# Layer two's node pass of a four-layer graph network: the reciprocal root of the variance from a ScalarE guess and two Newton steps on VectorE, in place of GpSimd's power

## The reference, cut to what matters

```python
def _layernorm(x, axis=-1, eps=1e-05):
    m = jnp.mean(x, axis=axis, keepdims=True)
    v = jnp.var(x, axis=axis, keepdims=True)
    return (x - m) / jnp.sqrt(v + eps)
...
    x = _layernorm(x + _L2_gnn_ref(x, src, dst, L2_gnn_W, L2_gnn_attn_l, L2_gnn_attn_r), axis=-1)
...
    # in _L2_gnn_ref: return jax.nn.elu(out.reshape(n, H * D))
    # in _L3_gnn_ref, the first steps:
    h = (x @ W.T).reshape(N, H, C)
    a_s = jnp.einsum('nhc,hc->nh', h, att_src)
    a_d = jnp.einsum('nhc,hc->nh', h, att_dst)
```

## Time and profile before

| | before |
|---|---|
| median of three runs, us | 5578.91 |
| lowest and highest, us | 5576.49, 5587.16 |
| profiled execution: span, us | 5581.5 |
| PE busy | 4162.6 us, 75% |
| DVE (VectorE) busy | 3702.1 us, 66% |
| POOL (GpSimd) busy | 3611.4 us, 65% |
| ACT (ScalarE) busy | 1962.3 us, 35% |
| power L1604 and scatters L1610 of the pass | 49 and 392 instructions |

### The profile page before, as it was taken

How to read it: one execution, slowest core, us unless ns; L and a number is a source line. 1 busy time by engine, 2 the same in 40 slices (tenths; PEclk the granted TensorE clock), 3 DMA queues, 4 the chain that set the end, 5 groups by cost and what they waited for, 6 DMA issues and landing times. The chain is left out here.

```text
span 5581.5 us, 69994 instructions
## 1 busy us (share of the span) xinstructions
PE 4162.6 (75%) x16758; PEld 2810.8 (50%) x16758; DVE 3702.1 (66%) x10203; ACT 1962.3 (35%) x3345; POOL 3611.4 (65%) x3319
## 2 busy tenths in 40 slices
PE   2276679999999999999999977776877500036666
PEld 1154445556666666666666667665666400012222
DVE  2155456666666666666666667777999665568887
ACT  0011135532222222222222222226888400026666
POOL 7488654443555556555555567775888777768887
PEclk7689889999999999999999988887999855569988
DMA  9988789985433333333333244447999733359998
GB/s 376 294 153 156 148 263 366 364 329 186 149 124 120 119 127 123 120 117 124 122 117 116 84 133 138 138 136 255 351 348 351 248 95 94 95 181 343 357 344 289
DMA packets 497175, 1129.62 MB, mean 202 GB/s; under 512 B 164007, under 2 KB 246907, under 8 KB 497031
## 3 DMA queue, kind: packets, MB, share of 16 engines
q1 hardware_dynamic: 331530, 866.20, 44.4%
q0 software_dynamic: 113184, 174.84, 12.9%
q10 hardware_dynamic: 52316, 87.06, 4.5%
HBM read 627.40 MB, written 543.83 MB: 210 GB/s over the span
## 5 line engine op out<-in xcount | busy, mean ns | idle before, releaser
L1067 PE MATMUL psum<-W2b,arena 128*128 128x256 f32 x3136 | 725.4, 380 | 0.0
L799 DVE TENSOR_SCALAR arena<-arena 128x256 f32<-128x256 f32 x784 | 462.6, 651 | 366.3 <-POOL arena L794 361.8
L1048 PE MATMUL psum<-arena,W1b 128*128 128x512 f32 x1568 | 699.2, 599 | 0.0
L1067 PEld LDWEIGHTS psum<-W2b,arena 128*128 128x128 f32 x3136 | 574.6, 191 | 65.2 <-issue 0.5
L1761 PE MATMUL psum<-arena,ident 128*128 128x512 f32 x784 | 409.9, 672 | 208.1 <-POOL arena L1819 206.0
L959 ACT ACTIVATE arena<-psum,hbias 128x512 f32<-128x512 f32 x392 | 269.4, 687 | 821.2 <-PE psum L1048 821.2
L1048 PEld LDWEIGHTS psum<-arena,W1b 128*128 128x128 f32 x1568 | 290.6, 190 | 401.7 <-issue 401.7
L1192 POOL DMA_INDIRECT tab<-arena,IDX x392 | 405.1, 1033 | 122.8 <-issue 91.5
L790 POOL TENSOR_TENSOR arena<-arena,lneps 128x4 f32<-128x4 f32 x196 | 41.5, 212 | 670.1 <-DVE arena L786 669.1
L1610 POOL DMA_INDIRECT ad_d<-arena,FE x392 | 394.6, 1007 | 114.3 <-issue 113.7
L917 POOL DMA_INDIRECT xd_d<-arena,FE x360 | 378.1, 1050 | 99.8 <-issue 96.9
(11 more groups left out here) (256 smaller groups left out, 9286.1 us busy)
## 6 DMA issues: line engine op xcount, KB each, us to landing
arena<-tab SPq DMA_DIRECT2D x194, 544.0 KB
arena<-x_d SPq DMA_DIRECT2D x202, 512.0 KB, 7.0
arena<-in_x SPq DMA_DIRECT2D x194, 512.0 KB, 4.8
x_d<-arena SPq DMA_DIRECT2D x194, 512.0 KB, 2.9
tab<-zero SPq DMA_DIRECT2D x11, 5832.0 KB, 54.9
tab<-blank SPq DMA_DIRECT2D x97, 544.0 KB
h_d<-arena SPq DMA_DIRECT2D x97, 528.0 KB, 6.0
arena<-h_d SPq DMA_DIRECT2D x97, 528.0 KB, 5.5
```

Source lines behind the costliest of these rows:

```text
L799: v.tensor_scalar(y[:, j, :], r[:, j, :], self.mv[:, j, 0:1], self.rs[:, j:j + 1], ALU.subtract, ALU.mult).then_inc(self.s["y"], 1)
L1048: last = pe.matmul(psum[:, HB[c], :], W1b[:, f, c * P:(c + 1) * P], x1T[:, f, :], start=False, stop=(f == FH - 1))
L1067: last = pe.matmul(outB(j), hid[:, c, j * P:(j + 1) * P], W2b[:, c, :], start=(c == 0), stop=(c == KH - 1))
```

## The change

The power leaves GpSimd. VectorE now writes `half` = (variance + epsilon) / 2 for a pair (in place of `ve`). ScalarE makes a first guess of the reciprocal root: it reads the bits of `half` as an integer, which is near a linear function of the logarithm, and takes the exponential of that times -ln 2 / 2^24 plus a constant `logb`. VectorE improves the guess in `shift` by two steps of the form r = r x (half x r x r - 1.5), three instructions each, every one waiting for the one before by the semaphore `small`. The sign turns with each step and is right after two. The semaphore counts of the last pass are moved to match.

```diff
--- before.py
+++ after.py
@@ -98,6 +98,9 @@
     BIG = 1.0e30
     LN_EPS = 1e-5
     SLOPE = 0.2
+    LN2 = 0.6931471805599453
+
+    LOGB = 0.5 * LN2 * (127 - 0.043 - 1.0)
 
     NS = -(-N // STEP)
     NLAST = (N - (NS - 1) * STEP) // J
@@ -1474,7 +1477,9 @@
             y = take([NB, J, D])
             st = take([J, 6])
             mv = take([2, 2 * J, 2])
-            ve = take([2 * J])
+            half = take([2, 2 * J])
+            t1 = take([2 * J])
+            logb = take([1])[:, 0:1]
             rsd = take([2, 2 * J])
             nm = take([2, 2 * J])
             gap = take([1])
@@ -1483,7 +1488,7 @@
             cursor[0] = max(cursor[0], ahead["edge_end", 2])
             xt = take([NB, J, D])
             unit = psum[:, 6:8, :].rearrange("p a (j d) -> p (a j) d", d=D)
-            r = dict(nodes, **nodes2)
+            r = dict(nodes, small=nodes3["small"], **nodes2)
             assert NS % 2 == 0 and NB == 4
 
             def out_wait(eng, k):
@@ -1581,9 +1586,16 @@
                     wait(act, r["mm"], 2 * (k.s - 1))
                     for f in range(FH):
                         act.activation(xT[:, k.slot(2), f, :], psum[:, f, :], ACT.Copy).then_inc(r["xT"], 1)
+                def guess(k):
+                    b = k.slot(NB) // 2
+                    act.wait_ge(r["ve"], k.turn(2) + 2)
+                    wait(act, r["nm"], k.turn(2) - 1)
+                    act.activation(rsd[:, b, :], half[:, b, :].bitcast(I32), ACT.Exp, bias=logb, scale=-LN2 / 2 ** 24).then_inc(r["rs"], 1)
                 relu_exp(beat(0, NB))
 
                 def body(k):
+                    if k.slot(2) == 0 and not (k.known() and k.s == 0):
+                        guess(k.plus(-2))
                     if live(k.plus(1), NS):
                         relu_exp(k.plus(1))
                     if not (k.known() and k.s < 2):
@@ -1591,18 +1603,13 @@
                     if not (k.known() and k.s < 3):
                         evac(k.plus(-3))
                 run_beats(act, NS, body, NB, peel=2 * NB)
+                guess(beat(NS - 2, NB))
                 for s in range(NS - 2, NS):
                     normed(beat(s, NB))
                     evac(beat(s - 1, NB))
                 evac(beat(NS - 1, NB))
 
             def n_gpsimd(pool):
-                def rstd(p):
-                    wait(pool, r["y"], J * (2 * p - 2))
-                    wait(pool, r["nm"], p - 1)
-                    pool.wait_ge(r["ve"], p + 1)
-                    pool.tensor_tensor(out=rsd[:, p % 2, :], in0=ve, in1=expo[:, :], op=ALU.pow).then_inc(r["rs"], 1)
-
                 def to_edges(k):
                     pool.wait_ge(r["hs"], 2 * (k.s + 1))
                     for j in range(J):
@@ -1610,8 +1617,6 @@
                         pool.indirect_dma_start(out=ad_d[:, :], out_offset=bass.IndirectOffsetOnAxis(ap=FE[:, c:c + 1], axis=0),
                                                 in_=hs[:, k.slot(NB), j, D + H3:HW], in_offset=None, bounds_check=EP - 1, oob_is_err=False).then_inc(s_xd[k.slot(NB)], 16)
                 for s in range(NS):
-                    if s % 2 == 1:
-                        rstd(s // 2)
                     if s > 4:
                         to_edges(beat(s - 5, NB))
                 for s in range(NS - 5, NS):
@@ -1631,9 +1636,16 @@
 
                 def shift(k):
 
-                    b = k.slot(NB) // 2
-                    v.wait_ge(r["rs"], k.turn(2) + 1)
+                    b, p = k.slot(NB) // 2, k.turn(2)
+                    v.wait_ge(r["rs"], p + 1)
                     wait(v, r["y"], J * (k.s - 2))
+                    for i in range(2):
+                        v.tensor_tensor(out=t1, in0=rsd[:, b, :], in1=half[:, b, :], op=ALU.mult).then_inc(r["small"], 1)
+                        v.wait_ge(r["small"], 6 * p + 3 * i + 1)
+                        v.tensor_tensor(out=t1, in0=t1, in1=rsd[:, b, :], op=ALU.mult).then_inc(r["small"], 1)
+                        v.wait_ge(r["small"], 6 * p + 3 * i + 2)
+                        v.scalar_tensor_tensor(out=rsd[:, b, :], in0=t1, scalar=-1.5, in1=rsd[:, b, :], op0=ALU.add, op1=ALU.mult).then_inc(r["small"], 1)
+                        v.wait_ge(r["small"], 6 * p + 3 * i + 3)
                     v.scalar_tensor_tensor(out=nm[:, b, :], in0=mv[:, b, :, 0], scalar=-1.0, in1=rsd[:, b, :], op0=ALU.mult, op1=ALU.mult).then_inc(r["nm"], 1)
 
                 def body(k):
@@ -1660,10 +1672,10 @@
                         v.bn_aggr(mv[:, k.slot(NB) // 2, b * J + j, :], st[:, j, :]).then_inc(r["mv"], 1)
                     if b == 1:
                         v.wait_ge(r["mv"], J * (k.s + 1))
-                        wait(v, r["rs"], k.turn(2))
-                        v.tensor_tensor(out=ve, in0=mv[:, k.slot(NB) // 2, :, 1], in1=lneps[:, :], op=ALU.add).then_inc(r["ve"], 1)
+                        v.tensor_scalar(half[:, k.slot(NB) // 2, :], mv[:, k.slot(NB) // 2, :, 1], LN_EPS, 0.5, ALU.add, ALU.mult).then_inc(r["ve"], 1)
                     if not (k.known() and k.s < 4):
                         to_rows(k.plus(-4))
+                v.memset(logb, LOGB).then_inc(r["ve"], 1)
                 run_beats(v, NS, body, NB, peel=NB + 1)
                 shift(beat(NS - 2, NB))
                 for s in range(NS - 4, NS):
@@ -1824,7 +1836,7 @@
                     pool.wait_ge(r["mv"], J * (k.s + Z + 1))
                     pool.tensor_tensor(out=ve, in0=mv[:, b, :, 1], in1=lneps[:, 0:J], op=ALU.add).then_inc(r["ve"], 1)
                     wait(pool, r["y"], J * (k.s + Z - 1))
-                    pool.wait_ge(r["ve"], k.s + ZP + 1)
+                    pool.wait_ge(r["ve"], k.s + ZP + 2)
                     pool.tensor_tensor(out=rsd[:, b, :], in0=ve, in1=expo[:, 0:J], op=ALU.pow).then_inc(r["rs"], 1)
                     pool.wait_ge(r["rs"], k.s + ZP + 1)
                     pool.wait_ge(r["neg"], k.s + 1)
@@ -1842,7 +1854,7 @@
                 def factors(k):
 
                     p = k.turn(2)
-                    c0 = 6 * p
+                    c0 = 6 * (p + ZP)
                     for n in (k, k.plus(1)):
                         b = n.slot(NB)
                         v.wait_ge(gd[b], 16 * (n.turn(NB) + GD[b] + 1))
```

## The result

The changed kernel takes 5613.78 us (median of four runs, 5605.57 to 5618.13) against 5583.03 us of the kernel before in the same comparison (5576.49 to 5588.44). The ratio is 1.0056 with an interval of 1.0041 to 1.0070: 31 us slower, between 23 and 39. The forecast was 5603, 24 more, in a range of 5590 to 5622. A second comparison gave 1.0055 (1.0041 to 1.0069). The profiled execution's span grew from 5581.5 to 5616.4 us.

What follows compares the result with a forecast made beforehand. The prediction took GpSimd to bound the changed pass, VectorE close behind. Steps +60.5, waits given back -29.3 and tail -7.2 sum to +24.0 us; on the median 5578.9 that gives 5603, range 5590 to 5622.

Steps and rivals of the forecast that it cites:

- The bound: In the changed pass's loop GpSimd never waits and sets the pace; VectorE has only 1.15 us to spare in four beats.
- The price of the steps: Six chained 128x8 VectorE instructions in front of L1637 for each of 48 pairs, 0.21 us each: +60.5 us.
- The waits given back: VectorE's waits for GpSimd's power in the changed pass disappear: -29.3 us.
- The tail: At the pass's end GpSimd is behind with its scatters; without the power they end earlier: -7.2 us.
- ScalarE and TensorE at 0: The guess's place in ScalarE's order makes neither evacuation nor matmuls late in the loop; slack about 1.0 us, cost 0.
- What was to be seen: Changed profile: turn about 25.9 us, steps 0.21 apart, GpSimd idle some 0.9 a beat, last scatter about 7 after last L1634.
- Rival A: The six steps flow like independent instructions, 0.07 us apart: not slower, -16 us, 5563; chance 6%.
- B: The loop's register instructions make each Newton step instruction cost 0.30 us: +50 us, 5629; chance 8%.
- C: The guess in ScalarE's order makes evacuation and matmuls late, so VectorE's L1629 waits: 48 us more, 5651; chance 7%.
- Rival D: VectorE's Newton steps and GpSimd's scatters hold each other in the loop: 125 us more, 5728; chance 2%.
- The argument against D: L1853, L1855 and L1858 start 0.22 to 0.23 us apart beside GpSimd's power, so instructions with two SBUF inputs aren't held.
- the likeliest case: Whole kernel with step pitches of 0.20 to 0.23 us (+21 to +30) and a tail gain of 5 to 8: 5598 to 5611.

## Why the prediction was right, and where it was not

- **The bound.** Right: GpSimd set the pace, VectorE had 1.15 us a turn to spare. The kernel without steps shows the 23.42 as 23.40.
- **The price of the steps.** 0.21 each was taken, 0.20 measured. 48 x 6 x 0.20 = 57.6 for 60.5: this term was 3 us too large and is most of what the pass fell short of the forecast. Taken by the kernel without steps it is 658.0 - 602.8 = 55.2. A turn was to be 25.94 and is 25.81.
- **The waits given back.** -29.3 fits: 57.6 - 29.3 - 6.4 (the tail, next point) = 21.9 for 21.3 measured. No run shows it alone. The kernel without steps shows it together with a tail: 602.8 - 636.7 = -33.9, where -29.3 - 7.2 = -36.5 was forecast. By that run this part was too large by 2.6 and the steps by 5.3, and the two errors cancel in part.
- **The tail.** From the last variance to the last scatter's end it was 4433.08 - 4399.28 = 33.8 us and is 4456.10 - 4428.65 = 27.5: -6.4 where -7.2 was forecast, and the gap between the last L1634 and the end is 8.2 for some 7. GpSimd started beat 93's scatters at 4430.85, 0.8 after L1634's end at 4430.08, where I had it start at once; a scatter of the beat before was under way until 4430.17. The kernel with the unused power takes 5.1 of the gain back.
- **ScalarE and TensorE at 0.** Right, and shown alone by the guess in the old kernel (635.9 against 636.7). The guess itself is 0.30, not the 0.23 of the nearest row.
- **What was to be seen.** Right but for GpSimd's idle time: it waits for L1634 43.1 us in the 36 beats of the stretch above, 1.2 a beat, where the text said 0.9; its own terms, 25.94 / 4 - 5.2, give 1.3.
- **Rival A** (0.07 apart) described instructions that don't depend on each other, and these exist: 0.077. The Newton steps are a chain and don't behave so. B and C did not occur. **Rival D** did not occur in this pass: the longest L1643 of 98 is 0.242 us, although more than half of the pass's small VectorE instructions start while a scatter runs.
- **The argument against D was wrong in its breadth.** From one place in the last pass I concluded that the trace disagrees with the Trainium skill ("SBUF — State Buffer", Who interferes with whom), by which a VectorE instruction with two SBUF inputs and a GpSimd one that reads SBUF exclude each other for a whole instruction. L1853 and L1855, two of the very lines I cited, are held for 1.8 us in the profile of before that was at hand (4963.75 and 4965.61), behind the product L1819. The rule agrees with the trace for that product. It does not for the power: in the last pass of that profile 314 VectorE instructions of 128x32 start beside one and take 0.193 (median), and with the unused power 15 of 128x8 start beside it and take at most 0.169. Nor does it for the scatters. The sum was not touched, as only these two run here.
- **The total.** 31 us for 24. The missing part is no term of the sum: the 10 us outside the changed pass, which the profiles place in the last pass. I priced its edits at nothing and left them unnamed among the risks; whether they are its cause is open. 5613.8 lies above the 5598 to 5611 of the likeliest case. That it is in the range is in part luck: the upper part of the range was meant for half of rival B and the spread of runs, and something else filled it.

## What to carry to other kernels

Before work is moved off the engine that sets the pace, read how much the next engine has to spare in one turn of the loop: the gap was 0.58 us a pair here, and a chain of six small instructions, 1.2 us, could not fit into it although each is tiny. Price small instructions by whether they wait for each other (0.20 us here) or not (at most 0.08), and shorten the chain or give each engine a part of the pairs rather than move all of it. An engine that comes out of a loop behind its work leaves a tail, and what waits at a fixed place in its order makes it fall behind even when it has time.

## What the runs showed of the hardware that was not expected

- Six VectorE products of 128x8 started 0.077 us apart when independent, and cost the loop only 0.035 each; in a chain they started 0.20 apart (0.193 without a register instruction between), at a duration of 0.17 each.
- A VectorE instruction of 128x32 with two SBUF inputs took 1.6 to 1.9 us in place of 0.19 beside GpSimd's 128x1024 product (1.9 us), until 0.05 us after that product's end; a few that started in its first 0.012 us or its last 0.06 took 0.18. Beside GpSimd's power (1.0 us on 4 columns in the last pass) it was not held, nor were those of 128x8 beside the power on 8 columns (1.6 to 2.1 us) and beside scatters.
- The last pass of one and the same kernel lasted 611 to 619 us in three profiles, while the changed pass repeated within 0.5.
- A chain's pitch of 0.227 us did not change with the level of the semaphore that it waits for (starting from 0, or from 294).
